# Third layer of a four-layer conditioned sequence kernel: the rotation's last product moved ahead of the turned q and k on TensorE, the MLP's residuals moved ahead of row norm and head norm on VectorE

## The reference

```python
mod = silu(c) @ w_mod + b_mod                       # six parts: shift, scale, gate, twice
xn  = ln(x) * (1 + sc_msa) + sh_msa
q, k, v = split(xn @ w_qkv + b_qkv)                 # 16 heads of 18
q, k = ln(q), ln(k)                                 # layers 1 and 3; layer 3 with scale and bias
o   = softmax(q k^T / sqrt(18)) v
x   = x + g_msa * (o @ w_proj + b_proj)
xn2 = ln(x) * (1 + sc_mlp) + sh_mlp
x   = x + g_mlp * (gelu(xn2 @ w1 + b1) @ w2 + b2)   # the MLP, 1152 wide
...
# after layer 3
z   = x @ U                                         # U: 288 x 64, from a QR factorisation
out = x + (z @ R - z) @ U^T                         # R = expm(A) of each sample, 64 x 64
```

## Time and profile before

| | |
|---|---|
| three timed runs, median | 5047.29 us (5041.9 to 5056.23) |
| profiled execution, its own time | 5031.73 us |
| its span, first to last instruction | 5029.7 us |
| mean granted TensorE clock | 0.936 |
| TensorE busy | 89% |
| VectorE busy | 72% |
| ScalarE busy | 46% |
| GpSimd busy | 23% |
| third layer, first to last `R_z` | 3475.8 to 5021.2 us |

### The profile page before, as it was taken

How to read it: one execution, slowest core, us unless ns; L and a number is a source line. 1 busy time by engine, 2 the same in 40 slices (tenths; PEclk the granted TensorE clock), 3 DMA queues, 4 the chain that set the end, 5 groups by cost and what they waited for, 6 DMA issues and landing times. The chain is left out here.

```text
span 5029.7 us, 125303 instructions
## 1 busy us (share of the span) xinstructions
PE 4485.4 (89%) x46073; PEld 3750.3 (75%) x46073; DVE 3636.1 (72%) x7659; ACT 2291.6 (46%) x3894; POOL 1134.3 (23%) x2045
## 2 busy tenths in 40 slices
PE   6764999999999978999999999958999999999998
PEld 4543788888888866888888888747777777777776
DVE  5665888888888855777776776657777777777774
ACT  1213555555555534444454554434445454445443
POOL 1002222222222222222222222222222212222211
PEclk7676999999999988999999999979999999999998
DMA  3002001100110111001011000110000001000000
GB/s 73 20 0 60 24 27 28 28 28 28 28 28 22 26 51 32 25 28 28 28 28 28 28 28 25 30 49 21 26 23 25 23 20 27 20 24 23 24 20 18
DMA packets 122230, 141.59 MB, mean 28 GB/s; under 512 B 14446, under 2 KB 117780, under 8 KB 122112
## 3 DMA queue, kind: packets, MB, share of 16 engines
q1 hardware_dynamic: 121968, 139.75, 10.2%
q10 hardware_dynamic: 144, 0.22, 0.0%
HBM read 110.87 MB, written 29.06 MB: 28 GB/s over the span
## 5 line engine op out<-in xcount | busy, mean ns | idle before, releaser
L867 DVE TENSOR_REDUCE mx<-S 128x4 f32<-128x1024 f32 x768 | 920.2, 1216 | 80.7 <-PE S L1105 77.8
L629 ACT ACTIVATE pT<-S 128x1024 f32<-128x1024 f32 x768 | 745.1, 1022 | 366.5 <-PE S L1131 362.1
L577 ACT ACTIVATE hf<-M 128x512 f32<-128x512 f32 (+1 forms) x480 | 266.5, 555 | 1161.1 <-PE M L1185 673.4
L504 POOL TENSOR_SCALAR hh<-hf 128x512 fp32r<-128x512 f32 (+1 forms) x480 | 276.6, 576 | 1174.7 <-ACT hf L577 1130.9
L1131 PE MATMUL S<-qT,kT 32*128 32x256 f32 x9216 | 425.8, 295 | 65.9 <-ACT pT L629 64.3
L1105 PE MATMUL S<-kT,qT 32*128 32x256 f32 x3072 | 368.8, 334 | 85.8 <-DVE mx L867 47.1
L1131 PEld LDWEIGHTS S<-qT,kT 32*128 32x128 f32 x9216 | 329.0, 185 | 138.0 <-ACT pT L629 93.2
L1144 PE MATMUL A<-pT,V 128*32 128x256 f32 x6144 | 413.5, 387 | 20.0 <-ACT pT L629 20.0
L858 DVE TENSOR_TENSOR hl<-hf,hh 128x512 fp32r<-128x512 f32 (+1 forms) x480 | 323.3, 675 | 111.9 <-POOL hh L504 110.0
L1185 PE MATMUL M<-xh,w_hi 128*128 128x256 f32 x1728 | 392.7, 310 | 3.3 <-POOL xh L480 3.3
L1105 PEld LDWEIGHTS S<-kT,qT 32*128 32x128 f32 x3072 | 222.8, 188 | 206.3 <-DVE mx L867 83.4
(11 more groups left out here) (231 smaller groups left out, 10118.2 us busy)
## 6 DMA issues: line engine op xcount, KB each, us to landing
mid<-xbo SPq DMA_DIRECT2D x64, 288.0 KB, 3.2
xld<-mid SPq DMA_DIRECT2D x64, 288.0 KB, 3.1
xa<-mid SPq DMA_DIRECT2D x64, 288.0 KB, 3.6
gA<-gates SPq DMA_DIRECT2D x96, 144.0 KB, 3.3
gM<-gates SPq DMA_DIRECT2D x96, 144.0 KB, 3.0
xld<-in_x_dram SPq DMA_DIRECT2D x32, 288.0 KB, 3.5
xa<-in_x_dram SPq DMA_DIRECT2D x32, 288.0 KB, 3.5
out_dram<-xbo SPq DMA_DIRECT2D x32, 288.0 KB, 2.2
```

The lines of the kernel that those rows point to most:

```text
L504: pool.tensor_scalar(hh[:, 2 * f:2 * f + m, :].rearrange("p m c -> p (m c)"), hf[:, f % 2, 0:m * T], 1.0, 0.0, ALU.mult, ALU.add).then_inc ...
L577: act.activation(hf[:, f % 2, 0:c], MBANK[f % 2][:, 0:c], ACT.Gelu if rot else ACT.Gelu_apprx_tanh).then_inc(s["m_hf"], 1)
L629: act.activation(pT[:, g % 2, 2 * h:2 * h + 2, :], S[:, 2 * h:2 * h + 2, :], ACT.Exp, scale=float(HD) ** -0.5).then_inc(s["a_ex"], 1)
L867: dve.tensor_reduce(mx[:, p, :, :], S[:, r:r + 2, :].rearrange("p a (t k) -> p a t k", t=NT), AX.X, ALU.max).then_inc(s["a_mx"], 1)
```

## The change

The change touches only the third layer (`rot`). On TensorE `R_out` moves ahead of `A_turn_qk`. On VectorE `M_x2(d, 0)` moves ahead of `M_norm(m)`, and `M_x2(d, 1)` moves ahead of `A_heads_norm(p)`, behind `A_heads_rstd(p)`. No instruction is added or removed, and each waits for what it waited for.

```diff
--- before.py
+++ after.py
@@ -961,13 +961,19 @@
                                 dve.wait_ge(v_lo, NCH * (layer + 1))
+                        if d is not None and rot:
+                            M_x2(d, 0)
+                        if m is not None:
                             M_norm(m)
-                        if d is not None:
+                        if d is not None and not rot:
                             M_x2(d, 0)
                         if p is not None and eps is not None:
                             A_heads_rstd(p)
+                        if d is not None and rot:
+                            M_x2(d, 1)
+                        if p is not None and eps is not None:
                             A_heads_norm(p, None)
-                        if d is not None:
+                        if d is not None and not rot:
                             M_x2(d, 1)
                         if nxt is not None:
                             A_xl(nxt)
@@ -1320,8 +1326,10 @@
                         if p is not None:
                             if a is None and layer == 0:
                                 pe.wait_ge(set_done, 14)
+                            if rot and d is not None:
+                                R_out(d)
                             A_turn_qk(p)
-                        if rot and d is not None:
+                        elif rot and d is not None:
                             R_out(d)
                         if a is not None:
                             A_turn_o(a)
```

## The result

| | before | changed |
|---|---|---|
| timed runs, median | 5041.88 us (5028.9 to 5056.23, 20 runs) | 5053.84 us (5044.13 to 5064.11, 20 runs) |
| profiled span | 5029.7 us | 5042.4 us |
| mean granted clock | 0.936 | 0.934 |

The ratio is 1.0023, with a 95% interval of 1.0013 to 1.0034: 12 us slower, in an interval of about 7 to 17. That is within the 0.3% that I called no change, and inside the range, but the central figure of +1.5 us lies outside the interval. The profiled executions agree: from the first `R_y` to the last the third layer takes 1544.5 us before and 1555.9 us changed, 11.4 more.

A forecast was written before the change was run, and what follows sets the result against it. TensorE sets the pace, its chain through VectorE and the low clock settling slots at 51.20 us. The straight sum, 29 x 0.5 = 14.5 us, is taken back by the clock, leaving +1.5: 5048.8 us, range 5037 to 5064.

The forecast's parts named there:

- the central figure of +1.5 us: Whole kernel: slide of 0.6 to 1.0 us once, plus 0.5 for an end slot that no longer settles; 5048.8 us.
- the second rival: Third-layer slots: settling is coincidence or slide limited, each slot 0.5 us longer; +14.5, at 0.7 each +20; chance 0.12.
- TensorE waits 0.5 us for `yT`, and nothing is given back for it: TensorE ahead of `R_out`: copy of `yT` no longer hidden, 0.5 us lost a slot, bounds 0 to about 0.7.
- VectorE's new wait of 2.0 us is covered: VectorE ahead of `M_x2(d, 1)`: waits 2.0 us, covered by the 3.77 us wait ahead of second `A_oraw`; cost 0.
- `R_x3` earlier returns nothing, because the second reciprocal waited for `A_turn_o`: VectorE: `R_x3` out of the way earlier, but second reciprocal waits for `A_turn_o`; gain at most 0.18 us.
- Low clock twice: Rival: clock also falls over transposes standing alone on TensorE; +0.5 to +1.7 us a slot, 5062 to 5097; chance 0.06.
- 50.63 is still below 51.20, so the slot settles at 51.20 again: Third-layer slot: own work rises from 50.13 to 50.63 us, clock loss falls from 1.07 to 0.57, length stays 51.20.
- also reaches the second scores and the eight products ahead of the `xl` wait: TensorE, slid position: low clock covers this work too, costs some and makes the slide up to 1.0 us.
- at 0.44: Dense TensorE products: each us at low clock loses 0.44 us, from 0.12 against 0.215 us a product.
- The work of before: Third-layer slot before the change: own work without the clock's loss, 51.20 - 1.07 = 50.13 us.
- the 1.07 that I had counted on: Clock loss in a slot before, over 2.42 us of dense products; the most the clock can give back.
- The first case: Third-layer slots: added 0.5 us absorbed by the clock, slots stay 51.20, +0 to +3 us overall; chance 0.72.

## Why the prediction was right, and where it was not

The range and the forecast of no change beyond 0.3% held: the ratio is 1.0023, and the time lies in 5037 to 5064. But one step on the way was wrong, and the forecast of no change held by luck: 12 us came where 1.5 were forecast, and 12 happens to be less than the 15 that I had called no change. The range held because it had been drawn up towards the second rival. Taken step by step:

- *TensorE waits 0.5 us for `yT`, and nothing is given back for it*: right in kind, a little large in size. The wait is 0.47, and the second scores come 0.39 later, where 0.5 had been carried through. TensorE's part alone gives the whole loss, and covering the copy again takes it away.
- *VectorE's new wait of 2.0 us is covered*: right, 2.00 us, with 2.46 left ahead of the second `oraw` (forecast 1.8 to 2.3, a little low). Alone it costs nothing.
- *`R_x3` earlier returns nothing, because the second reciprocal waited for `A_turn_o`*: right. The wait moved to the first reciprocal (1.87 us).
- *Low clock twice*: not over the transposes, which is what this rival named. They run from 4100.54 to 4104.04 in the slot shown, and the clock falls only at 4107.74, by the 51.20 spacing from 3851.74. A double low stretch did come, in the slots to which the sliding had led. The Trainium skill, "TensorE: Matmul & The Clock Gate", in its part 4 on the PE-mode transpose, says that a transpose doesn't count as busy in the same way for the clock gate. These slots don't bear that out: 3.5 us of transposes run at full clock, and it stays up for 3.7 us behind them.
- *"50.63 is still below 51.20, so the slot settles at 51.20 again"*: this step failed. The work did slide, and the low stretch moved from 10.0 us behind `R_y`'s start towards 9.3, as forecast (9.0 to 9.4 us). But the slot did not get shorter than 51.31 us. I had written that the low clock "also reaches the second scores and the eight products ahead of the `xl` wait ... which costs some"; that "some" is the term that was too small. In the slot shown, the scores take 0.59 us to the next start instead of 0.43, the eight products 1.87 us, and the products with `xl` restart 11.75 us behind `R_y` instead of 10.97: set by TensorE itself and no longer by the wait for VectorE. From the second scores' start to the restart that is 2.46 us instead of 2.07, a loss of 0.39 (by chance as much as the scores come later); behind it the low clock lasts to 4111.15, 1.13 us of dense products, at 0.44 a loss of 0.50. By this estimate the clock cost 0.89 us in the slid place, and I had let it fall to 0.57. The work of before, the later scores and this loss, 50.13 + 0.39 + 0.89, make 51.41, near the 51.31 measured. So the slot stayed 0.11 above 51.20, and the slide never ended. In slots with one low stretch the clock took back 0.28 of the 0.39 us, not up to the 1.07 that I had counted on; with 0.27 us of added products it took back all but 0.02, and with 0.53 the shortest slot was 51.45, again 0.28 taken back. Then the double stretches cost it again: on average 0.39 made 0.40, and 0.53 made 0.91.
- In the terms of the forecast, what happened is the second rival, "the slide is limited", to which I gave 0.12, and at 0.40 us a slot instead of 0.5: 29 x 0.40 = 11.6 us, where 12.0 were measured. The first case, with 0.72, did not happen. The second rival's reason held, its sum was too large: it let 0.5 us through to each slot.

That the slots settle to the spacing of the clock's changes is shown by the cut of two products, whose slots stayed at 51.20 while the low stretch moved by 0.6 us in the slot, and by the two added ones. Why some double stretches come in a row with four more products, and what in detail makes a stretch come or stay away, is left open.

## What to carry to other kernels

When a product that reads a freshly copied result is moved ahead, look for what had covered the copy: here 0.38 us of ScalarE's copy had been hidden by transposes, and putting the product between them covers the copy again. Here a wait of 2 us on an engine with a longer wait behind it cost nothing, and work that ended earlier on an engine that then waited for another gained nothing.

Where a loop's length is the same to 0.01 us while the low clock comes once in each turn, small savings and costs may not show: find the work ahead of the low stretch and try to shorten the waits there until the stretch disappears. That paid 2.9 us a slot, of which 1.1 was the clock.

## What the runs showed of the hardware that I had not expected

- Work taken from a steady loop can gain nothing at all: with 0.27 and with 0.53 us less of 51.2, the mean of the steady slots stayed 51.20 us. With 0.53 us more it grew by 0.91, and where the clock stays up, the same products cost 0.56.
- A low stretch can be followed at once by another of the same length: 6.8 us instead of 3.4, which made slots of 52.8 us among slots of 51.3.
